# A second graph layer whose 24 boundary sums read saved rows instead of gathering again

## What is computed

```python
m     = clifford_linear(h_src * r_uv, msg_w, msg_b)   # h_src = h[src], r_uv = relation_emb[type]
m     = m * gate[:, :, None] * norm[:, None, None]
h_agg = jax.ops.segment_sum(m, dst, num_segments=num_nodes)
h_out = clifford_linear(h_hc + h_agg, upd_w, upd_b)
```

## Time and profile before

| | |
|---|---|
| three runs | 3828.66, 3844.82, 3862.87 us |
| median | 3844.82 us |
| profiled execution: span from the first to the last instruction | 3293.4 us |
| its own time outside that span | not listed; the median is 551.4 us over the span |
| busy: PE, VectorE, ScalarE, POOL | 2474.5, 1533.4, 1429.7, 1972.5 us |
| share of the span | 75%, 47%, 43%, 60% |
| mean granted clock of PE | 0.840 |
| second graph layer's sums | 1656.7 to 2729.2 us of the span |

### The profile page before, as it was taken

One profiled execution on the slowest core, in us unless ns is written; L12 is line 12 of the kernel. 1 busy time (PEld: TensorE's weight loads), 2 busy tenths in 40 slices (PEclk: granted clock), 3 DMA queues, 4 the chain that ended last, 5 costly groups with the idle time before them and its releaser, 6 DMA issues. The chain is left out here.

```text
span 3293.4 us, 52336 instructions
## 1 busy us (share of the span) xinstructions
PE 2474.5 (75%) x14033; PEld 1893.1 (57%) x14033; DVE 1533.4 (47%) x4471; ACT 1429.7 (43%) x3654; POOL 1972.5 (60%) x1945
## 2 busy tenths in 40 slices
PE   1569999999999849874066666666766677499997
PEld 1236666778888738763034444444444446499996
DVE  6668889722211241003756556666665665511110
ACT  0257676557710113322454444444444443255553
POOL 2537777677777267655477777777777770133332
PEclk9989999999999859997577776667666767699998
DMA  6647666688887455674477777777777761464233
GB/s 220 227 128 208 201 210 198 204 267 263 264 254 240 132 178 179 194 234 138 125 220 205 203 206 204 205 201 206 201 206 205 205 186 52 152 193 103 43 80 64
DMA packets 366585, 609.37 MB, mean 185 GB/s; under 512 B 82338, under 2 KB 231979, under 8 KB 363536
## 3 DMA queue, kind: packets, MB, share of 16 engines
q1 hardware_dynamic: 261984, 334.64, 31.8%
q0 software_dynamic: 100208, 265.56, 30.5%
q10 hardware_dynamic: 4144, 6.20, 0.5%
HBM read 443.45 MB, written 167.60 MB: 186 GB/s over the span
## 5 line engine op out<-in xcount | busy, mean ns | idle before, releaser
L658 POOL DMA_INDIRECT agg_r_rows<-h_table,parts_and_x x832 | 836.7, 1006 | 289.4 <-issue 209.1
L714 PE MATMUL agg_r_sums<-agg_r_rows,agg_r_onehot 128*128 128x257 f32 x1664 | 689.1, 562 | 368.0 <-DVE agg_r_rows L696 318.4
L1412 POOL DMA_INDIRECT rl_buf<-r_table,kinds x632 | 649.5, 1028 | 263.1 <-issue 174.9
L714 PEld LDWEIGHTS agg_r_sums<-agg_r_rows,agg_r_onehot 128*128 128x128 f32 x1664 | 418.5, 276 | 619.9 <-issue 538.1
L625 ACT ACTIVATE agg_r_gap<-iota,parts_and_x 128x128 f32<-128x128 f32 x832 | 286.8, 392 | 459.9 <-PE agg_r_sums L714 433.6
L687 DVE TENSOR_TENSOR acc<-acc,agg_r_sums 128x257 f32 (+1 forms) x836 | 353.5, 423 | 152.2 <-issue 64.8
L696 DVE TENSOR_TENSOR agg_r_rows<-agg_r_rows,agg_r_rel 128x514 f32<-128x514 f32 x416 | 290.5, 698 | 282.0 <-DMA agg_r_rows<-h_table,parts_and_x 280.3
L1810 PE MATMUL f_pH<-f_xT,f_w 128*128 128x128 f32 x2816 | 352.1, 283 | 27.4 <-DMA f_w<-in_L_ffn_w 17.3
L1810 PEld LDWEIGHTS f_pH<-f_xT,f_w 128*128 128x128 f32 x2816 | 338.1, 197 | 57.2 <-issue 21.4
L1180 PE MATMUL ly_acc<-matrix_and_parts 128*128 128x256 bf16 x1250 | 341.7, 273 | 0.0
L1829 PE MATMUL f_pY<-f_w,f_hT 128*128 128x256 f32 x1408 | 327.9, 383 | 16.7 <-DMA f_w<-in_L_ffn_w 16.6
(11 more groups left out here) (397 smaller groups left out, 3519.8 us busy)
## 6 DMA issues: line engine op xcount, KB each, us to landing
agg_r_rel<-relation_rows SPq DMA_DIRECT2D x404, 260.0 KB, 3.2
relation_rows<-rl_buf SPq DMA_DIRECT2D x316, 260.0 KB, 4.5
relation_rows<-f_rr_buf POOLq DMA_DIRECT2D x60, 260.0 KB, 3.1
f_w<-in_L_ffn_W SPq DMA_DIRECT2D x28, 512.0 KB, 5.7
f_w<-in_L_ffn_W SPq DMA_DIRECT2D x14, 1024.0 KB
agg_r_rows<-h_table,parts_and_x POOLq DMA_INDIRECT x832, 3.4
ly_zin<-zh SPq DMA_DIRECT2D x50, 256.0 KB, 4.5
zh<-ly_out SPq DMA_DIRECT2D x50, 256.0 KB, 2.8
```

What stands on the lines that cost most here:

```text
L658: pool.indirect_dma_start(rows[:, n % SLOTS, t, :], None, table, bass.IndirectOffsetOnAxis(ap=indices[:, t:t + 1], axis=0)).then_inc(s_row ...
L714: last = nc.tensor.matmul(sums[:, (2 * n + t) % BANKS, 0:used], onehot[:, n % HOT, t, :], rows[:, n % SLOTS, t, 0:used], start=True, stop= ...
L1412: pool.indirect_dma_start(self.buf[:, n, g, :], None, self.table, bass.IndirectOffsetOnAxis(ap=self.c.kinds[:, at:at + 1], axis=0)).then_i ...
```

## The change

ScalarE copies every multiplied half (128x257) into `saved`, 26 slots of 257 columns, one per node tile, by the half's own tile number. Later halves of a tile overwrite earlier ones, so that at the end each slot holds the tile's last half, the one that the next tile's boundary cuts. The 24 extra sums take their rows from there: `again` reads the half's number from `b_start`, its tile from `b_tile`, and gives PE that slot. `saved` takes the place of `xn` in SBUF (somewhat larger; `xn` is now a view of it). `b_start` now holds the number of a half instead of that of a row. The copies are written into `places`: those of block n - 5 stand in `places(n)`. `Beside`'s work on ScalarE is put off by five blocks as well. PE waits for `s_save` (a count of the copies) where it waited for `s_ready`. Gathers, loads and multiplications now end with block 403.

```diff
-                v.tensor_scalar(at[:, 0, :], starts, bits, bits, ALU.arith_shift_right, ALU.logical_shift_left)
...
+                def keep(half):
+
+                    at = half + 2 * LAG
+                    tile = act.value_load(c.tab["b_tile"][0:1, at:at + 1], min_val=0, max_val=NT)
+                    n, t = divmod(half, 2)
+                    act.wait_ge(s_ready, n + 1)
+                    if half:
+                        act.wait_ge(s_save, half)
+                    nc.scalar.activation(saved[:, bass.ds(tile, 1), :].rearrange("p a d -> p (a d)"), rows[:, n % SLOTS, t, 0:used], ACT.Copy)\
+                        .then_inc(s_save, 1)
+
                 def places(n):
-                    g = n
+                    g, older = n, n - (HOT - 1)
 
                     act.wait_ge(s_sum, g + (SLOTS + 2 - HOT))
                     for t in range(2):
                         last = nc.scalar.activation(gap[:, n % HOT, t, :], c.iota[:, 0:P], ACT.Abs, bias=c.tab["b_near"][:, bass.ds(g * 2 + t, 1)])
                     last.then_inc(s_gap, 1)
+                    if 0 <= older < BLOCKS:
+                        keep(2 * older)
                     act.wait_ge(s_gap, g + 1)
                     nc.scalar.activation(onehot[:, n % HOT, :, :], gap[:, n % HOT, :, :], ACT.Relu, bias=1.0, scale=-1.0).then_inc(s_oh, 1)
+                    if 0 <= older < BLOCKS:
+                        keep(2 * older + 1)
...
-                    beside.scalar(act, n)
+                    beside.scalar(act, n - (HOT - 1))
...
-                for n in range(total):
+                for n in range(BLOCKS):
                     gather(n, c.tab["b_src"][:, n * 2:n * 2 + 2])
...
-                def sum_up(g, n):
-                    pe.wait_ge(s_acc, 2 * (g + LAG + 1))
-                    pe.wait_ge(s_oh, g + 1)
-                    pe.wait_ge(s_ready, g + 1)
+                def again(n, t):
+
+                    at = 2 * (n - BLOCKS) + t
+                    half = pe.value_load(c.tab["b_start"][0:1, at:at + 1], min_val=0, max_val=HALVES - 1)
+                    tile = pe.value_load(c.tab["b_tile"][0:1, bass.ds(half + 2 * LAG, 1)], min_val=0, max_val=NT)
+                    return saved[:, bass.ds(tile, 1), :].rearrange("p a d -> p (a d)")
+
+                def sum_up(n):
+                    terms = [rows[:, n % SLOTS, t, 0:used] if n < BLOCKS else again(n, t) for t in range(2)]
+                    pe.wait_ge(s_acc, 2 * (n + LAG + 1))
+                    pe.wait_ge(s_oh, n + 1)
+                    pe.wait_ge(s_save, min(2 * n + 2, HALVES))
                     for t in range(2):
-                        last = nc.tensor.matmul(sums[:, (2 * n + t) % BANKS, 0:used], onehot[:, n % HOT, t, :], rows[:, n % SLOTS, t, 0:used],
-                                                start=True, stop=True)
+                        last = nc.tensor.matmul(sums[:, (2 * n + t) % BANKS, 0:used], onehot[:, n % HOT, t, :], terms[t], start=True, stop=True)
                     last.then_inc(s_sum, 1)
...
-        c.xn = c.sb("xn", [P, NT, D])
+        c.saved = c.sb("xn", [P, (NT + 1) * (D + 1)])
+        c.xn = c.saved[:, 0:NT * D].rearrange("p (t d) -> p t d", d=D)
```

More of the change, by code:

```diff
@@ L479, in _ @@
                 sp.wait_ge(s_row, 1)
-                sp.dma_start(c.tab["b_start_d"], at[:, 0, :]).then_inc(s_saved, 16)
+                sp.dma_start(c.tab["b_start_d"], at[:, 1, :]).then_inc(s_saved, 16)
                 sp.wait_ge(s_near, 1)
@@ L602, in aggregate @@
     total = BLOCKS + EDGES_AT // 2
+    saved = c.saved[:, :].rearrange("p (t d) -> p t d", d=used)
     with Core(nc) as k:
@@ L610, in aggregate @@
         s_rows = [c.pool_sem(f"{name}_rows{s}") for s in range(SLOTS)]
-        s_gap, s_oh, s_ready, s_sum, s_acc, s_gate = (k.sem(f"{name}_{x}") for x in (
-            "gap", "onehot", "ready", "sum", "acc", "gate"))
+        s_gap, s_oh, s_ready, s_save, s_sum, s_acc, s_gate = (k.sem(f"{name}_{x}") for x in (
+            "gap", "onehot", "ready", "save", "sum", "acc", "gate"))
         with nc.Block() as block:
@@ L643, in _ @@
                     sp.dma_start(rel[:, n % SLOTS, :, :], src).then_inc(s_rel[n % SLOTS], 16)
[L644 to L649, removed]
             @block.gpsimd
@@ L666, in _ @@
                 v = nc.vector
-                def loads_of(n):
-                    slot = [q for q in range(n + 1) if q % SLOTS == n % SLOTS]
-                    return sum(16 if q < BLOCKS else 32 for q in slot)
                 def tile_of(half):
@@ L692, in _ @@
                 for n in range(total):
[L693 to L696, removed]
+                    if n < BLOCKS:
+                        dve.wait_ge(s_rel[n % SLOTS], (n // SLOTS + 1) * 16)
+                        dve.wait_ge(s_rows[n % SLOTS], (n // SLOTS + 1) * 32)
+                        here = rows[:, n % SLOTS, :, 0:used]
+                        v.tensor_tensor(here, here, rel[:, n % SLOTS, :, 0:used], ALU.mult).then_inc(s_ready, 1)
                     add(n)
@@ L707, in _ @@
                 last.then_inc(s_sum, SLOTS + 1)
-                def sum_up(g, n):
-                    pe.wait_ge(s_acc, 2 * (g + LAG + 1))
-                    pe.wait_ge(s_oh, g + 1)
-                    pe.wait_ge(s_ready, g + 1)
+                def again(n, t):
[8 more added lines that the diff above has]
+                    pe.wait_ge(s_save, min(2 * n + 2, HALVES))
                     for t in range(2):
-                        last = nc.tensor.matmul(sums[:, (2 * n + t) % BANKS, 0:used], onehot[:, n % HOT, t, :], rows[:, n % SLOTS, t, 0:used],
-                                                start=True, stop=True)
+                        last = nc.tensor.matmul(sums[:, (2 * n + t) % BANKS, 0:used], onehot[:, n % HOT, t, :], terms[t], start=True, stop=True)
                     last.then_inc(s_sum, 1)
                 for n in range(total):
-                    sum_up(n, n)
+                    sum_up(n)
                     beside.tensor(pe, n)
```

## The result

The changed kernel takes 4360.77 us (median of 4 runs, 4330.72 to 4372.56), the kernel before 3853.85 us (median of 4, the three shown earlier and one more). The ratio is 1.1312, with a 95% interval of 1.126 to 1.1363: **slower by 13%, some 507 us**. The forecast was 4475 us, with a range of 4330 to 4600.

What follows compares the result with a forecast made beforehand. POOL's gathers were taken to bound the stage before, a ScalarE-PE ring the changed one. 404 x 4.18 us plus smaller terms made 1,706 us against 1,073, so 3844.8 + 633 = about 4475 us, range 4330 to 4600.

Steps and rivals of the forecast that it cites:

- The ring: In the 404 blocks with copies, ScalarE and PE take turns, the six blocks of slack gone; 404 x 4.18 = 1,689 us.
- Its length: Period per block: 0.04 + 1.95 + 0.14 + 2.05 = 4.18 us at the lower clock, bounds 3.88 and 4.48.
- PE's clock: PE at the lower level for nearly all of the stage: a sum takes 2.05 us, against 1.10 at the upper.
- The stretches that were to raise the clock: 25 times the four `be_result` matmuls behind a sum keep PE going, each giving back 0.95 us on one or two sums: -36 us.
- The register loads in the ring: ScalarE's register load before each copy: 280 ns, 0.73 us from start of the load to the copy.
- rival B: Register loads slower beside busy engines, 0.60 us each: 404 x 0.64 = 259 us more, 4734 us; chance 0.06.
- The last 12 blocks: Without gathers, at PE's pace with its register loads: 2.3 us a block, 28 us where before it was 31.
- The stage after the change: All sums with the change, including start, ScalarE's other work and what the clock gives back: 1,706 us.
- The stage before: The 416 sums of the kernel before, 2.58 us a block, led by POOL's gathers: some 1,073 us.
- the missing 551 us: Median of three runs, 3844.82 us, lies 551 us above the profiled span of 3293.4; what lies around it left as is.
- Work removed: 24 of 832 gathers, 24 loads on SP's queue and 12 VectorE multiplications gone; last 12 blocks 28 us against 31.

Runs made afterwards that it cites:

- lag 4: Changed kernel with the copies of block n - 4 instead of n - 5 in `places(n)`: 3965.31 us, 1.025 of the kernel before.
- lag 2: Changed kernel with the copies of block n - 2 instead of n - 5 in `places(n)`: 3961.55 us, 1.0273 of the kernel before.
- eight slots: Changed kernel with eight one-hot slots instead of six and 11 row slots instead of 12, copies still five blocks late: 3970.23 us, 1.03 of the kernel before.
- ring with 11 row slots: Changed kernel with 11 row slots in place of 12 and nothing else: 4344.96 us, 1.1257 of the kernel before.
- filled ring: Changed kernel with seven bf16 matmuls of zeros per block on PE before its wait for the copy: 4017.5 us, 1.0415 of the kernel before.
- ordinary execution: Kernel before, unchanged, timed and profiled once more: 3859.44 us, ratio 1.0028, span of the profiled execution 3826.7 us.
- loads alone: Kernel before with three unread register loads and their checks added per block on ScalarE: 3908.13 us, 1.0143 of the kernel before.
- work removed alone: Changed kernel without its 808 copies and their register loads, PE waiting for `s_ready`: 3873.39 us, 1.0041 of the kernel before.
- fixed slots two blocks late: Changed kernel with copy slots n mod 25, no register load per copy, and copies of block n - 2 in `places(n)`: 3878.78 us, 1.0045 of the kernel before.
- shorter loads: Changed kernel with copies of block n - 2 in `places(n)` and tile numbers read without the run-time check: 3883.52 us, 1.0069 of the kernel before.

## Why the prediction was right, and where it was off

**The ring** (right). The forecast: `places(n)` waits for sum n - 6, sum n - 5 waits for copies written behind that wait, and so ScalarE and PE take turns. The timeline shows it, and two different edits that widen the difference between 6 and 5 (lag 4 and 2; eight slots) open it: lag 4 and lag 2 for 395 and 399 us, eight slots for 375 against the ring with 11 row slots (4345 - 3970).

**Its length** (right, 2% too long). Forecast 4.18 us, measured 4.09. Gap to copy 0.70 where I took 0.77, one-hot to copy 0.42 where I took 0.44. End of the copy to PE 0.14, PE to ScalarE 0.04, as taken. 404 x 0.09 = 36 us.

**PE's clock** (right). Taken: the lower level for nearly all of it; measured 0.53. The filled ring shows that the level was the price: sums of 1.13 us instead of 2.05, and 343 us less. The stretches that were to raise the clock did: it rose 25 times in the ring, each time within 5 us of a start of `be_result`'s matmuls, and fell again each time. 16 whole sums ran in 1.1 us; all that was given back is some 26 us, where 36 were taken. The rule of the Trainium skill in TensorE: Matmul & The Clock Gate, section HAM oscillation — how this bites in real kernels, which ties the fall to long idle gaps, is not borne out here: before none of these falls was PE idle for more than 2.34 us at a time.

**The register loads in the ring** (right in kind). 280 ns from an experts' line, 276 in this layer (272 to 296 for all 808); rival B with its 0.60 us falls. The Trainium skill, page DMA: Bandwidth & Descriptors, section Latency and other measured facts, has about 600 ns as the floor of a tensor_load; for these loads the trace does not agree.

**The last 12 blocks** (too cheap). Taken 2.3 us each; from 3763.7 to 3801.2 us they took 3.1. The four loads of a block, one after the other with their checks, run on PE's list from 3767.1 to 3769.9 us, and its first matmul starts at 3770.22: they are only partly hidden. 10 us.

**The stage after the change** came out at 1,687 us, forecast 1,706.

**The stage before** (the step that failed). The forecast put the missing 551 us around the span and said: "I leave what lies around it as it is". An ordinary execution has nothing of note around it (span 3826.7 us, time 3828.41). The sums of an ordinary execution take 1,193 us, not 1,073, so the difference is smaller by 120 us: 633 - 120 = 513, measured 507. The forecast stage was nearly right because its errors are small and partly cancel: 36 us too much for the period, 10 too little for the last blocks, and 10 too much given back by the clock. The range was made for errors of 0.30 us in the period and one in the clock, not for this one; that the time still fell inside it, 31 us above its lower end, is in part luck.

**Work removed** (right that it is little, wrong in its sign). 3 us were forecast as gain in the last blocks. They take 37.5 us with the change and 21.2 in the ordinary execution before, so the new loads on PE cost some 16 us there. The whole of it alone gives 1.0041 (1.0003 to 1.008), no gain.

**How the 507 us come apart,** step by step as the experiments take them away: opening the ring 4361 - 3962 = 399; then the longer list of instructions on ScalarE 3962 - 3879 = 83; then the copies 879 - 873 = 5 (of 3879 and 3873), which is nothing. Some 20 are left (3873 - 3854): about 10 of them are the chip, on which the kernel before took 3863, and 10 are the 1.0041 of the work removed. These are steps along one path and not parts of the changed kernel's time. In that kernel slow instructions hardly occur (2 in 1,687 us), and the ring alone makes its stage longer; that they take the ring's place when it is opened is what lag 4 and lag 2 show. The middle step was not in the forecast; rival B had slow register loads, but all 808 of them and inside the ring.

**Still open.** That the slow register instructions are ScalarE waiting for its own code is likely: two blocks late, their number and the loss go with the length of its list (15 instructions a block: 548 and 1.027; 11: 308 and 1.007; 7: none and 1.0045). And in a slow stretch of lag 2 (2696 to 2704 us) loads, checks and waits alternate between 0.01 and 0.7 us whatever they do, some two of them every 0.7 us. But no record shows the delivery of code as what they wait for: the page of the profile counts 171 packets on queue 14, of kind "instruction", for lag 2 and 172 for the changed kernel. Nor is the length all of it, since loads alone (12 a block) have 570 slow ones and cost half as much as lag 2 with its 15. VectorE has such instructions too, 56 in the ordinary execution before and 67 to 85 with the work removed alone, with fixed slots two blocks late and with shorter loads, but 0 to 11 where ScalarE has 495 or more and none in the ring; which engine suffers is not explained. Why the first profiled execution was free of them is open too.

## What to carry to other kernels

Where an engine's instruction waits for block n - a, and work is written behind it on which block n - b depends, the two close a ring of a - b blocks; count that difference before busy times, since ScalarE's were only 45% in the ring (765 of 1,688 us). Keep b well below a; to put the late work ahead of the wait should do the same, but was not tried. And set a profile's span against its time: where they are far apart, that profile can be of another kind of execution than the runs, and its stage times are then not theirs.

## What had not been expected of the hardware

- The same program ran once in a span of 3293.4 us, and all its timed runs took 3824 to 3888 us. In the four windows above ScalarE is busy 1,302 us in the one and 1,296 in the other, PE 2,317 and 2,353; the difference lies in idle time, 358 us of it in the first graph layer. There POOL's wait for the transfers into `relation_rows` is 345.4 us where it was 86.3, and 177.9 us of the weight loads' idle time at L1167 have no engine named. Why is open.
- Register instructions that take 0.02 to 0.3 us at the median can take up to 1.40 us. There were some 500 such on ScalarE where its list was about 15 instructions per 3.2 us, but 2 at 4.09 us and, in the filled ring, 1 at 3.2 us. Their rate alone does not explain them.
- Seven matmuls of zeros per block made a kernel 343 us faster: PE's mean clock in the sums was 0.97 with them and 0.53 without.
